# Second block's feed-forward stages: the second bias by GpSimd on the residual instead of by matmuls

## What is computed

```python
x = x + 0.5 * _L0_ffn_ref(_layernorm(x), ...)      # two windowed attention layers with gated FFN
x = x + _L0_attn_ref(_layernorm(x), ...)           # causal linear attention
x = x + 0.5 * _L0_ffn_ref(_layernorm(x), ...)      # the same two layers again
x = x + 0.5 * _L1_ffn_ref(_layernorm(x), W1, b1, W2, b2)
x = x + _L1_attn_ref(_layernorm(x), ...)           # gated linear attention
x = x + 0.5 * _L1_ffn_ref(_layernorm(x), W1, b1, W2, b2)

def _L1_ffn_ref(x, W1, b1, W2, b2):                # Wq: weights rounded to -1, 0, 1
    h = relu(x @ Wq1.T + b1)
    return h @ Wq2.T + b2                          # 256 -> 1024 -> 256
```

## Time and profile before

| | us |
|---|---|
| median of three runs | 3194.92 |
| span of the profiled execution | 3193.4 |
| PE busy | 3068.6 (96%) |
| DVE busy | 2350.6 (74%) |
| ACT busy | 1729.0 (54%) |
| POOL busy | 1622.9 (51%) |
| first ternary pass (first to last of its groups, about) | 2735 to 2865 |
| second ternary pass | 3050 to 3193 |

### The profile page before, as it was taken

How to read it: one execution, slowest core, us unless ns; L and a number is a source line. 1 busy time by engine, 2 the same in 40 slices (tenths; PEclk the granted TensorE clock), 3 DMA queues, 4 the chain that set the end, 5 groups by cost and what they waited for, 6 DMA issues and landing times.

```text
span 3193.4 us, 99022 instructions
## 1 busy us (share of the span) xinstructions
PE 3068.6 (96%) x35586; PEld 2681.3 (84%) x35586; DVE 2350.6 (74%) x6543; ACT 1729.0 (54%) x4532; POOL 1622.9 (51%) x1839
## 2 busy tenths in 40 slices
PE   6999999999999999999899999989999899999889
PEld 5888878878887888998788878878888788888778
DVE  6888767677776787777777767767777688777766
ACT  4767642266767224665667672237767622454445
POOL 7777730177776224333777761037777444317610
PEclk9999999999999999999999999999999999999999
DMA  4211121021111101000211112102111200100001
GB/s 135 67 45 44 37 81 33 23 63 40 36 40 39 42 20 43 11 10 21 58 40 36 40 39 76 30 26 66 37 39 34 72 21 13 27 0 1 1 14 40
DMA packets 178774, 122.82 MB, mean 38 GB/s; under 512 B 27533, under 2 KB 175337, under 8 KB 178025
## 3 DMA queue, kind: packets, MB, share of 16 engines
q1 hardware_dynamic: 177432, 117.77, 13.8%
q10 hardware_dynamic: 1104, 1.90, 0.2%
HBM read 48.29 MB, written 20.98 MB: 22 GB/s over the span
## 4 chain that ended last, share of the span: by engine, by line
PE 87%; DVE 6%; issue 3%; POOL 1%; ACT 1%; DMA 1%; SPq 0%; DVEq 0%; POOLq 0%; ACTq 0%
PE bank L347 15%; PE bank L348 13%; PE bank L349 13%; PE bank L511 8%; PE bank L480 6%; PE bank L452 3%; PE bank L732 2%; PE bank L731 2%; PE bank L730 2%; PE bank L724 2%; PE bank L725 2%; PE bank L489 2%; PE bank L676 2%; PE bank L675 2%; PE bank L490 2%
## 5 line engine op out<-in xcount | busy, mean ns | idle before, releaser
L2652 POOL TENSOR_TENSOR prob<-prob,rsum 128x384 f32<-128x384 f32 x512 | 416.2, 834 | 155.8 <-DVE rsum L1861 155.8
L1209 ACT ACTIVATE prob<-prob,nmax 128x192 f32<-128x192 f32 x1024 | 455.8, 454 | 2.2 <-DVE nmax L1854 2.2
L1401 ACT ACTIVATE gate<-bank,bias 128x512 f32<-128x512 f32 x192 | 132.4, 690 | 512.0 <-PE bank L349 511.9
L2639 POOL TENSOR_TENSOR rn<-ss,mhalf 128x16 f32<-128x16 f32 x128 | 375.9, 2937 | 10.7
L1854 DVE CUSTOM_DVE_ANT_0 prob<-bank,masks,rn 128x192 f32<-128x192 f32 x768 | 275.1, 414 | 100.1 <-PE bank L480 99.3
L2646 POOL TENSOR_TENSOR qk<-rot_t 128x512 f32<-128x512 f32 x256 | 331.9, 1297 | 23.3 <-DVE ss L1828 21.3
L347 PE MATMUL bank<-wqkv_hi,hT_hi 128*128 128x512 f32 x768 | 329.5, 429 | 14.7 <-DVE rot_t L1816 6.1
L2620 POOL TENSOR_TENSOR rstd<-meanvar,eps 128x4 f32<-128x4 f32 x48 | 12.4, 259 | 620.4 <-DVE meanvar L1786 620.4
L348 PE MATMUL bank<-wqkv_lo,hT_hi 128*128 128x512 f32 x768 | 303.0, 395 | 0.0
L349 PE MATMUL bank<-wqkv_hi,hT_lo 128*128 128x512 f32 x768 | 302.8, 394 | 0.0
L347 PE MATMUL bank<-gT_hi,w_hi 128*128 128x512 f32 x704 | 277.2, 394 | 2.6 <-issue 2.6
(11 more groups left out here) (292 smaller groups left out, 9831.1 us busy)
## 6 DMA issues: line engine op xcount, KB each, us to landing
Vlo<-V SPq DMA_DIRECT2D x256, 64.0 KB, 2.0
Vhi<-V SPq DMA_DIRECT2D x256, 64.0 KB, 2.0
H<-Y SPq DMA_DIRECT2D x128, 64.0 KB, 1.8
H<-ya SPq DMA_DIRECT2D x128, 64.0 KB, 1.8
yb<-Y SPq DMA_DIRECT2D x128, 64.0 KB, 1.6
HB<-Y SPq DMA_DIRECT2D x32, 256.0 KB, 2.8
HB<-yb SPq DMA_DIRECT2D x32, 256.0 KB, 3.1
raw<-in_L_ffn_wqkv SPq DMA_DIRECT2D x4, 1536.0 KB, 8.3
```

The source lines that it names most:

```text
L1209: ins = e.activation(pb, pb, ACT.Exp, bias=nm[r][:, x:x + 1], scale=-1.0, accum_out=sums[r][:, x:x + 1])
L2639: e.tensor_tensor(rn[u][:, :], ss[:, :], mhalf[:, :], ALU.pow).then_inc(s_plRN, 1)
L2652: e.tensor_tensor(pair, pair, rs[:, 2 * gi:2 * gi + 2].unsqueeze(2).to_broadcast([P, 2, KW]), ALU.mult).then_inc(s_plPN[gi], 1)
```

## The change

GpSimd gets a new step `bias_added(n)` in both ternary passes: when `Xn` of group n is written, it adds `brow` to the four tiles of X of that group, in place, one instruction of 128x1024. It stands behind `ffn_stats(n + 1)` in GpSimd's program. `brow` is halved once, by GpSimd in pass 3 behind its group 0. VectorE waits for the add before it adds the second layer's result to X (`s_plXB`). The bias matmuls, `bias_rows`, `bone` and TensorE's wait for them are gone; the first matmul of the second layer opens the bank. `brows` remains as an unused piece of memory; `bone` (512 bytes a partition) does not, so the buffers that were allotted behind it move.

```diff
@@ tensor_program, w2_
-                    if joined and c == 0 and isinstance(n, int) and n == 0:
-                        e.wait_ge(s_prepV, cnt['V'] + 5 + OFF)
-                        e.wait_ge(s_prepB, cnt['B'] + 2 + OFF)
...
                         if not l0:
-                            if opens:
-                                e.matmul(acc[u // 2][:, :], bone[:, :], brows[:, :], start=True, stop=False, skip_group_check=True)
-                            e.matmul(o, hidh[:, c % RING, lt], raw2_r[:, :, c * P:(c + 1) * P], start=False, stop=False, skip_group_check=True)
+                            e.matmul(o, hidh[:, c % RING, lt], raw2_r[:, :, c * P:(c + 1) * P], start=opens, stop=False, skip_group_check=True)
@@ vector_program, w2_
                         else:
+                            if u == u0:
+                                e.wait_ge(s_plXB, G - GRP * NRUN + 1 + OFF)
                             e.scalar_tensor_tensor(v, o, 0.5, v, ALU.mult, ALU.add).then_inc(s_dvYB, 1)
...
-                def bias_rows():
-                    two = brow[:, :].unsqueeze(1).to_broadcast([P, 2, D])
-                    pair = brows[:, :].rearrange('p (a c) -> p a c', a=2)
-                    e.wait_ge(s_small, cnt['small'] + OFF)
-                    e.tensor_copy(pair, two).then_inc(s_prepV, 1)
-                    e.wait_ge(s_prepV, cnt['V'] + 4 + OFF)
-                    e.tensor_tensor(pair[TAILG:P], two[TAILG:P], pair[TAILG:P].bitcast(F32), ALU.subtract).then_inc(s_prepV, 1)
...
-                    if ternary and first:
-                        bias_rows()
@@ gpsimd_program, ffn
+                def bias_added(n):
+                    e.wait_ge(s_dvXN, U * (G0 + n + 1) + OFF)
+                    e.wait_ge(s_prepB, cnt['B'] + 2 + OFF)
+                    x = X[:, bass.ds(U * n, U), :]
+                    e.tensor_tensor(x, x, brow[:, :].unsqueeze(1).to_broadcast([P, U, D]), ALU.add).then_inc(s_plXB, 1)
+
                 def group(n, last):
                     if not last and not (not l0 and isinstance(n, int) and n == 0):
                         ffn_stats(pas, l0, n + 1)
                     elif ternary:
                         ffn_stats(NRUN, False, 0)
                     if ternary and n:
                         cut(n - 1)
+                    if not l0:
+                        bias_added(n)
...
                 if ternary:
                     e.memset(ones[:, :], 1.0).then_inc(s_prepB, 1)
-                    e.memset(bone[:, :].bitcast(F32), 1.0 / TAILG).then_inc(s_prepB, 1)
                 group(0, False)
+                if ternary:
+                    e.wait_ge(s_small, cnt['small'] + OFF)
+                    e.tensor_scalar(brow[:, :], brow[:, :], 0.5, None, ALU.mult).then_inc(s_prepB, 1)
```

More of the change, by code:

```diff
@@ L142, in build @@
         zrow = HB[0:B, 0, 0:P]
-        bone = sb("bias_one", [P, P], F32R)
         Vleft = [[sb(f"V{n}{i}", [P, INNER]) for n in ("lo", "hi")] for i in range(2)]
@@ L173, in build @@
         w1_h, w1_l = sb("w1_hi", [P, KD, (2 * CH - 1) * P], F32R), sb("w1_lo", [P, KD, (2 * CH - 1) * P], F32R)
-        brows = sb("bias_rows", [P, 2 * D], F32R)
+        sb("bias_rows", [P, 2 * D])
         w2_h = sb("w2_hi", [P, CF, D], F32R)
@@ L309, in build @@
         g_peU, g_acXN, g_plO, g_dvU = sem("g_peU"), sem("g_acXN"), sem("g_plO"), sem("g_dvU")
-        g_plBO = sem("g_plBO")
+        g_plBO, s_plXB = sem("g_plBO"), sem("s_plXB")
         everything = [s_prepV, *s_x, s_raw, s_lndvST, s_lndvAG, s_lnplRV, s_lndvXN, s_lnsST, s_prepA, s_prepB, s_small, s_raw2,
@@ L321, in build @@
                       g_acK, g_peKK, g_dvC, g_peQ, g_acQ, g_peO, g_dvS2, g_dvA2, g_acO, g_plR2, g_peU, g_acXN, g_plO,
-                      g_dvU, g_plBO]
+                      g_dvU, g_plBO, s_plXB]
         def spare(run, T):
@@ L647, in loads_F @@
                 prep['P'] += 1 + CF
-                prep['V'] += 5
+                prep['V'] += 3
                 prep['B'] += 2 + 2 * CF
```

## The result

| | before | after |
|---|---|---|
| median of the runs, us | 3195.23 (3190.87 to 3195.73) | 3228.28 (3225.19 to 3231.62) |
| after / before, 95% interval | | 1.0108 (1.0093 to 1.0122) |
| span of the profiled execution, us | 3193.4 | 3227.8 |
| forecast, us | | 3225 (3205 to 3238) |

The changed kernel is 33 us slower, 3 more than forecast. A second set of runs beside it gave 3226.95 against 3195.13, 1.0103 (1.0087 to 1.0118); its profiled span was 3224.0, 30.6 above that of before.

A forecast was written before the change was run, and what follows sets the result against it. TensorE was taken as packed, its groups delayed by late Xn: twelve at 1.64 us (19.7) less 1.4 gained, plus 11.9 for half clock, gave +30.2 on 3194.9, so 3225 us, range 3205 to 3238.

The forecast's parts named there:

- spells: Stretches of 3.4 us with TensorE's granted clock at 0.50 behind its waits; 7 of 12 taken, 1.7 us lost each.
- The order: In groups 1 to 6 of each pass the add starts when rstd ends, 0.48 us before VectorE starts the next Xn.
- Rival (a): Adds hidden, bias matmuls gained: 3188, if GpSimd takes over 0.5 us between rstd and add or Xn isn't held; chance 0.09.
- Late by 2.14: Xn of the next group is held by the GpSimd add: 2.44 less 0.30, so 2.14 us late.
- Free time 0.50: Lateness of Xn in a steady group that costs TensorE's transposes nothing: 0.55 - 0.05 = 0.50 us.
- Wait 2.10: TensorE's wait for Xn per held group: 2.14 - 0.50 + 0.46 = 2.10 us.
- Bias matmuls worth nothing in the held groups: Each of twelve groups ends 1.64 us later whatever the bias matmuls cost; TensorE merely waits 0.46 longer.
- The clock: TensorE's clock falls to half behind 7 of the twelve waits: +11.9 us, bounds 0 to 20.4.
- VectorE as the bound: Rival (d): VectorE at 14.6 us doesn't reach the period of 16 to 18; held hid_lo could add 4 us.
- What was counted at nothing: Removal of bias_rows, bone's memset and its wait, and halving brow on GpSimd: 0, or 0.7 us without cover for the halving.
- The sum: Held groups less gains +18.3, half clock +11.9, together +30.2 us on 3194.9.
- an Xn that isn't held: Second way to rival (a): Xn passes beside the GpSimd add and only hid_lo is held; chance 0.02.

The follow-up runs named there:

- the last kernel: In the changed kernel, each add waits for the next group's Xn, the last for hid_lo of chunk 6 of group 6; 3191.36 against 3195.13, ratio 0.9986.

## Why the prediction was right

It was right in sign, place and size: forecast 3225, measured 3228.28 and 3226.95. Two errors cancelled in it and the number of spells was luck. By its steps:

- **The order (right).** The add starts with the end of rstd, ahead of Xn, in all twelve groups. In two of them it is a hid_lo that it holds, with nearly the same wait (1.88 and 1.89), so ten first Xn take 2.5, not twelve. Rival (a) needed over 0.5 us between rstd and add; there is none.
- **Late by 2.14 (3.44 - 1.38 = 2.06 measured).** The add itself is 2.39 where nothing holds it, not the 2.44 of the merge. The 2.83 of the steady groups contains the hid_lo that it waited for.
- **Free time 0.50 (about 0.4).** I took 0.05 between the end of Xn and the transposes, from the join; in a steady group it is 0.14 (3157.01 + 3.44 = 3160.45, against 3160.59). The two errors cancel: a period of 18.05 against 18.0.
- **Wait 2.10 (2.10, which the row gives as 1.94).** From start to start the transposes come 3160.59 - 3158.26 = 2.33 behind the last matmul, and its pitch is 0.23. The row counts from the end of that matmul's stated length, 0.40. The waits of 2.55, 2.27 and 1.63, beside which I laid the 2.10, are counted as the row does; the right one to lay beside them was 1.94, midway between 1.63 and 2.27.
- **Bias matmuls worth nothing in the held groups (right).** With them or without, the period is 18.05. The kernel without adds shows their worth alone: 7.2 against the 6.9 of rival (a), though 0.38 a steady group and not 0.46, since Xn is then the limit.
- **The clock: 7 spells of 1.7 (7 of 1.56).** The number was a choice between bounds of 0 and 12 that no row decides, so that it is exact is luck; two executions agree on it. A spell costs 19.61 - 18.05 = 1.56. At the join one was 6.8 long in the first execution, which cost 1.1 that the forecast doesn't have, and 3.4 in the second.
- **VectorE as the bound (rightly left out).** It is busy for 14.45 in 18.05, and the held hid_lo cost no group anything: 18.05 contains no 0.3 more.
- **What was counted at nothing (right).** bias_rows and the halving of brow lie in pass 3, between the transposes at 2547.4 and those at 2721.9; this stretch takes 174.5 in both kernels. The memset of bone lay in the group ahead of it, where the 0.6 above arose; the kernel with zeros added, which keeps it, has 18.14 there, within what the kernels without it have. The halving itself took 1.08 and 0.88 in the two executions, not 0.7.
- **The sum.** The forecast was +30.2 on the span. Measured are +34.4, of which 3.8 arose ahead of any changed instruction, and +30.6 in the second execution. Without the spells the second leaves about 19.7, where the forecast had 18.3, and its spells come to 10.9, where it had 11.9.

**The step that was wrong** is the reading of a rule. I wrote that Xn doesn't run at a double rate, because it takes 0.40 for 256 columns where a cast takes 0.42 for 512. The runs show 0.14 for 256 further columns and 0.12 for the two scalars: it does. So does the cast: at the 0.26 for 256 columns of the two-input instructions its 512 columns alone would take 0.52. "SBUF — State Buffer", section "Who interferes with whom", of the Trainium skill lists tensor_scalar and cast among the operations that can take both of VectorE's ports, and says that such an instruction, or one with two SBUF inputs beside a GpSimd instruction that reads SBUF, contends with GpSimd, and that the later one is blocked. With the right rate the page and the trace agree in three places: Xn and hid_lo (two inputs) are held; a memset, which reads nothing, still holds Xn by 0.61; and the layer norm's statistics, with one SBUF input and not among the operations listed, pass. For the last, DVE and POOL of the changed kernel in the first layer norm's stage:

```profile
86.96 1.40 DVE L1706 BATCH_NORM_STATS2 stats<-X 128x6 f32<-128x256 f32 x4
87.63 1.28 POOL L2632 TENSOR_TENSOR qk<-rot_t 128x512 f32<-128x512 f32 x1
```

Four statistics take 1.40 in all with a GpSimd add of 1.28 over them (this line takes 0.40 to 0.42 for one in the whole trace), where four rows of the layer norm, at a double rate, took 2.40 beside such an add. In one place the two differ: beside GpSimd's one-input instruction VectorE is not blocked to its end. Under the 3.20 above the four Xn took 2.87 in all, and the first was done after 1.13. The forecast didn't suffer from the wrong reading, since it went by the rows; but I gave "an Xn that isn't held" a chance of 0.02 for a reason that doesn't exist.

What stays open: why the same wait of 1.9 is followed by half clock in some groups and not in others; why GpSimd's one-input instruction lets VectorE in between and the two-input one doesn't; and whether the 3.4 us between the profiled execution (3188.0) and the median (3191.4) of the last kernel are more than the scatter of the stretch named there.

## What to carry to other kernels

Before you add a GpSimd instruction with SBUF operands, look at what VectorE starts in the time that it would run, and whether TensorE waits for that; on a semaphore that is long satisfied it will start at the worst moment as readily as at a good one. Give it a wait that puts it behind the urgent instruction, and check the last group, which has no successor. Work removed from an engine that then waits is worth nothing, and may cost: here it lengthened twelve waits from 1.5 to 1.9, and seven of them were then followed by half clock. And the free time of a deadline shrinks by whatever is taken out of the queue that meets it: 0.46 taken out of TensorE's group gave 0.38.

## What the runs showed of the hardware

- A GpSimd add of 128x1024 (2.39 alone) made a VectorE instruction of 0.41 take 2.47, and one of 128x512 with two inputs (0.69) take 2.69. A GpSimd memset of 1024 columns (0.95) made it take 1.02 to 1.16, though the memset reads nothing.
- Small instructions of the two engines alternate: 0.81 to 0.83 for each Xn beside adds of 256 columns. Splitting the add in four made the hold only 0.40 shorter (3.04 against 3.44).
- GpSimd's one-input instruction of 128x1024 (3.20) made four Xn late by 1.49 only; the two-input one of 2.39 made them late by 2.06.
- TensorE, full before and after, waited 1.24 to 1.60 us sixty times (five kernels, twelve each), and the granted clock stayed at 1.00 behind all of them. Behind 24 waits of 1.88 to 1.97 (two executions of the changed kernel) it fell to 0.50 fourteen times, for 3.4 us, at 1.56 us each. At the join it fell behind a wait of 1.86 in one kernel and stayed at 1.00 behind one of 1.88 in another.
- Two per-partition scalars in place of two constants cost a VectorE tensor_scalar 0.12 (0.40 against 0.28 for 256 columns).
